# Composite convolution as three half-length products by column parity, with the differences and filter sums on VectorE

## The chip, the cores and the metric

One core of one Trainium2 chip. The metric is the device time in microseconds of one execution, launch to end; lower is better. The profile is of one execution of the same program.

## The reference, cut to what matters

`x` is (32 samples, 64 channels, 1024), `cond_512` a style vector of 128 per sample. Two levels follow each other, each a chain of four modulated convolutions over the columns, then a feed-forward part, with a residual:

```
for i, typ in enumerate(('same', 'upsample', 'same', 'downsample')):
    s = style @ mw[i].T + mb[i]                       # (B, 64) per layer
    weight = SCALE * w[i] * s[:, None, :, None]
    demod = rsqrt(sum(weight ** 2, axis=(2, 3)) + EPS)
    out = conv(out, weight * demod, typ) + b[i]       # 3 taps; blur by [1,3,3,1]/8 after up, before down
level 0: x1 = h + 2 * sum_k gate_k * B_k (A_k h)      # 64 adapters of rank 16, top 16 by a router, softmax gates
level 1: out = x1 + (h @ dequantised int4 weight) + bias
```

In both levels `h` stands for the conditioned tensor that enters the feed-forward part; the residual is taken from the level's input. All is float32 in the reference.

## The kernel before, in words

Columns are stored by parity: row p of a pair tile holds the 512 even and then the 512 odd columns. 32 samples make 16 pairs (`NPAIR`); a pair has samples a = 0 and 1. Channels are 64 (`C`), so 128 partitions are 64 channels x 2 column parities, and H = 512 is the length of a half row.

A product keeps float32 accuracy by splitting both operands in a high and a low part (`hi`, `lo`) and adding hi x hi, hi x lo and lo x hi: `products`, L168 to L175, three matmuls for each stationary tile. The high part is a ScalarE copy to fp32r, the low part a VectorE subtraction (`low`, L156 to L158).

The first convolution of a sample is `pe_layer1` (L620): 6 matmuls of 512 columns. ScalarE scales its result in PSUM and makes `h_hi` (`act_layer1`, L630), VectorE makes `h_lo` (`dve_layer1`, L639). The other three convolutions, with the two blurs, are folded per sample into one filter of 4 tiles: `pe_fold3` (L537) and `pe_fold2` (L571) compute the filters, `act_fold2` (L586) and `dve_fold2` (L598) make `e_hi` and `e_lo` and copy them to the other half of the partitions. `pe_cond` (L645) is the composite convolution: 4 tiles x 3 = 12 matmuls of 512 columns per sample, each tile against `h` shifted by one more column. `act_cond` (L654) scales it, adds the bias and writes the two edge columns, which come from a small side computation (`edge_tensor`, `edge_vector`) done once per level for all samples.

The work is ordered by hand, one program per engine, with semaphores between them. In the first level's step i (`first_step`, L1070, L1177, L1268) the convolutions of pair i + 1 are laced between the feed-forward matmuls of pair i: layer1, transposes (`pe_turn`), fold3, scores, 24 hidden matmuls, fold2, 24 hidden matmuls, convolution of sample 0, transposes of the gated tensor, convolution of sample 1, 48 adapter-output matmuls. In the second level's step (L1115 to L1127, L1220, L1330) there are 32 matmuls of `pe_quant` in place of them. VectorE's order in the second level is: fold-start lows, lows of the turned tensor, `h_lo` of sample 0, fold3 lows, `h_lo` of sample 1, reduction, `e_lo`, split of the next input (`dve_split`), row sum, residual. GpSimd adds the bias to the residual in the second level (L1040) and issues the stores of finished pairs and the loads of the residual's input. SyncE loads the input of a pair (`sp_load`, L931) as soon as the pair before has been split.

Each engine goes through its program strictly in order; a wait holds everything behind it on that engine. The start of each level (filters, tables, edges, and at level 0 the splitting of the adapter matrices) is straight code before the loops, in which pairs 0 and 16 are done, and pair 1 in an unrolled first step.

## Time and profile before

| | us |
|---|---|
| median of 3 runs | 992.88 |
| lowest and highest | 990.76, 996.49 |
| the profiled execution, its own time | 990.33 |
| its span, first to last instruction | 988.8 |
| mean granted TensorE clock in it | 0.978 |

Busy times are per engine; a matmul's duration includes its way through the array, so the spacing of starts, not the mean duration, is what one costs in a row of them. "Idle before" is the time in which the engine did nothing ahead of an instruction, and "<-" names what ended it. PEclk is the granted clock of TensorE: 1.00 is 2.4 GHz, 0.50 is 1.2 GHz. PE is TensorE, DVE VectorE, ACT ScalarE, POOL GpSimd, SP SyncE.

### The profile page before, as it was taken

The numbers are of one execution on the slowest core, as the hardware profiler recorded it, in microseconds if no ns is written. First come the engines' busy times: TensorE is split into PE (matmuls) and PEld (weight loads), VectorE is DVE, ScalarE is ACT, GpSimd is POOL, SyncE is SP. The second block draws the span as 40 slices with busy tenths as digits, with TensorE's granted clock in tenths as the row PEclk, the third lists the DMA queues.
The fourth block names the chain that finished last, engine by engine and source line by source line (L and its number), as shares of the span: only waits on it lengthen the run. The fifth ranks groups of instructions, "written<-read, shape, count | busy, mean of one in ns | idle before, by whom it ended". The sixth has DMA issues, their size and how long they took to land.

```text
span 988.8 us, 14065 instructions
## 1 busy us (share of the span) xinstructions
PE 940.2 (95%) x4636; PEld 792.4 (80%) x4636; DVE 558.3 (56%) x1133; ACT 376.2 (38%) x717; POOL 111.0 (11%) x141
## 2 busy tenths in 40 slices
PE   5899999999999999999999998839999999999997
PEld 4777888888888888888888887638888888888886
DVE  8894353353353354344344333966677767777774
ACT  2672243243243243233233221434554445444541
POOL 7100000000000000000000000710112111211121
PEclk8799999999999999999999999859999999999999
DMA  8701011011011011101101101331221222112211
GB/s 281 244 5 65 22 42 64 21 42 64 21 42 64 25 39 64 40 25 63 42 28 57 42 21 54 54 106 29 100 85 64 65 96 94 64 64 87 96 50 64
DMA packets 33567, 64.12 MB, mean 65 GB/s; under 512 B 12304, under 2 KB 13968, under 8 KB 33552
## 3 DMA queue, kind: packets, MB, share of 16 engines
q1 hardware_dynamic: 24480, 30.90, 10.6%
q0 software_dynamic: 9072, 33.03, 9.2%
q8 instruction: 7, 0.11, 0.0%
q14 instruction: 8, 0.07, 0.0%
HBM read 47.14 MB, written 16.78 MB: 65 GB/s over the span
## 4 chain that ended last, share of the span: by engine, by line
PE 88%; DVE 8%; issue 2%; ACT 1%; DMA 1%; POOL 0%; SPq 0%; POOLq 0%; DVEq 0%; ACTq 0%
PE conv_ps L172 9%; PE conv_ps L174 8%; PE conv_ps L173 8%; PE fold_ps L581 6%; PE prod_ps L743 6%; PE prod_ps L744 6%; PE prod_ps L745 6%; PE prod_ps L725 6%; PE prod_ps L726 6%; PE prod_ps L727 6%; PE prod_ps L824 6%; PE prod_ps L823 6%; PE fold_ps L548 3%; PE turn_ps L682 3%; PE turn_ps L704 1%
## 5 line engine op out<-in xcount | busy, mean ns | idle before, releaser
L158 DVE TENSOR_TENSOR h_lo<-conv_ps,h_hi 64x512 fp32r<-64x512 f32 x128 | 88.2, 689 | 47.3 <-ACT h_hi L637 46.4
L172 PE MATMUL conv_ps<-h_hi,e_hi 128*128 128x512 f32 x256 | 104.9, 410 | 2.4 <-issue 2.4
L657 ACT ACTIVATE cond<-conv_ps,bias,demod_tab 128x510 f32<-128x510 f32 x64 | 49.9, 779 | 144.7 <-PE conv_ps L174 132.7
L173 PE MATMUL conv_ps<-h_lo,e_hi 128*128 128x512 f32 x256 | 102.2, 399 | 0.0
L174 PE MATMUL conv_ps<-h_hi,e_lo 128*128 128x512 f32 x256 | 102.1, 399 | 0.0
L743 PE MATMUL prod_ps<-b_hi,xt 128*128 128x512 f32 x256 | 99.9, 390 | 2.3 <-DVE xt L158 2.3
L823 PE MATMUL prod_ps<-quant,xt_hi 128*128 128x512 f32 x256 | 100.3, 392 | 1.4 <-DVE xt_lo L158 1.4
L801 DVE SCALAR_TENSOR_TENSOR res<-prod_ps,norm,res 128x512 f32<-128x512 f32 x32 | 23.9, 750 | 137.3 <-PE prod_ps L745 137.3
L726 PE MATMUL prod_ps<-a_lo,xt 128*128 128x512 f32 x256 | 101.0, 395 | 0.0
L725 PE MATMUL prod_ps<-a_hi,xt 128*128 128x512 f32 x256 | 101.0, 394 | 0.0
L727 PE MATMUL prod_ps<-a_hi,xt 128*128 128x512 f32 x256 | 101.0, 394 | 0.0
L824 PE MATMUL prod_ps<-quant,xt_lo 128*128 128x512 f32 x256 | 100.2, 391 | 0.0
L744 PE MATMUL prod_ps<-b_lo,xt 128*128 128x512 f32 x256 | 99.6, 389 | 0.0
L745 PE MATMUL prod_ps<-b_hi,xt 128*128 128x512 f32 x256 | 99.6, 389 | 0.0
L688 ACT ACTIVATE xt<-turn_ps 128x512 fp32r<-128x512 f32 x32 | 17.4, 594 | 166.8 <-PE turn_ps L682 166.8
L158 DVE TENSOR_TENSOR xt<-turn_ps,xt 128x512 fp32r<-128x512 f32 x64 | 41.3, 686 | 60.5 <-ACT xt L755 45.1
L1020 POOL DMA_DIRECT2D x_after_first<-res x15 | 8.1, 537 | 512.8 <-DVE res L801 512.8
L172 PEld LDWEIGHTS conv_ps<-h_hi,e_hi 128*128 128x128 f32 x256 | 49.2, 192 | 12.9 <-issue 2.5
L743 PEld LDWEIGHTS prod_ps<-b_hi,xt 128*128 128x128 f32 x256 | 48.0, 188 | 12.7 <-DVE xt L158 2.7
L755 ACT ACTIVATE xt<-turn_ps 128x512 fp32r<-128x512 f32 x32 | 17.6, 596 | 106.4 <-PE turn_ps L734 106.4
L174 PEld LDWEIGHTS conv_ps<-h_hi,e_lo 128*128 128x128 f32 x256 | 48.9, 191 | 11.5
L173 PEld LDWEIGHTS conv_ps<-h_lo,e_hi 128*128 128x128 f32 x256 | 49.1, 192 | 10.2
(222 smaller groups left out, 1982.4 us busy)
## 6 DMA issues: line engine op xcount, KB each, us to landing
x_in<-in_x SPq DMA_DIRECT2D x64, 128.0 KB, 2.7
res<-in_x POOLq DMA_DIRECT2D x16, 512.0 KB, 3.6
x_after_first<-res POOLq DMA_DIRECT2D x16, 512.0 KB, 2.9
x_in<-x_after_first SPq DMA_DIRECT2D x64, 128.0 KB, 2.7
res<-x_after_first POOLq DMA_DIRECT2D x16, 512.0 KB, 3.5
out_x<-res POOLq DMA_DIRECT2D x15, 512.0 KB, 2.9
a_raw<-in_adapter_in SPq DMA_DIRECT2D x8, 512.0 KB, 8.1
b_raw<-in_adapter_out SPq DMA_DIRECT2D x8, 512.0 KB, 8.0
```

Of the source, the lines that this page charges most:

```text
L158: return nc.vector.tensor_tensor(out, whole, hi.bitcast(F32), ALU.subtract)
L172: nc.tensor.matmul(out, hi(w), moving_hi(i), start=(i == 0), stop=False)
L173: nc.tensor.matmul(out, hi(w), moving_lo(i), start=False, stop=False)
L174: last = nc.tensor.matmul(out, lo(w), moving_hi(i), start=False, stop=(i == n - 1))
L725: nc.tensor.matmul(prod_ps[n][:, :], bufs.xt_hi[:, k, :], bufs.a_hi[:, k, cols], start=(k == 0), stop=False)
L726: nc.tensor.matmul(prod_ps[n][:, :], bufs.xt_hi[:, k, :], bufs.a_lo[:, k, cols], start=False, stop=False)
L727: last = nc.tensor.matmul(prod_ps[n][:, :], bufs.xt_lo[:, k, :], bufs.a_hi[:, k, cols], start=False, stop=(k == KT - 1))
L743: nc.tensor.matmul(prod_ps[n][:, :], bufs.xt_hi[:, k, :], bufs.b_hi[:, k, cols], start=(k == 0), stop=False)
L744: nc.tensor.matmul(prod_ps[n][:, :], bufs.xt_hi[:, k, :], bufs.b_lo[:, k, cols], start=False, stop=False)
L745: last = nc.tensor.matmul(prod_ps[n][:, :], bufs.xt_lo[:, k, :], bufs.b_hi[:, k, cols], start=False, stop=(k == KT - 1))
L823: nc.tensor.matmul(prod_ps[n][:, :], bufs.xt_hi[:, k, :], bufs.quant[:, k, cols], start=(k == 0), stop=False)
L824: last = nc.tensor.matmul(prod_ps[n][:, :], bufs.xt_lo[:, k, :], bufs.quant[:, k, cols], start=False, stop=(k == KT - 1))
```

## The change

The composite convolution of a sample, 4 filter tiles over 512 columns, becomes three products of 2 filter tiles over 256 columns each. The result of layer1 is scaled into one scratch buffer in SBUF by column parity: even columns as "centre", odd columns as "odd". VectorE forms two differences, odd - centre and (odd by one) - centre, of 257 columns each. ScalarE copies the 771 columns of differences and centre to `h_hi`, VectorE takes the low part. The filters are built whole (not split) in a scratch that overlaps that data buffer, VectorE adds neighbouring filters (two sums), ScalarE makes the high and VectorE the low part of six tiles. TensorE computes the middle product (filter sums against the centre) into `fold_ps[a]` and the two others (filters against the differences) into the halves of `conv_ps[a]`. ScalarE scales the middle product and adds the bias, and VectorE joins: the two halves times the scale, plus the middle, written interleaved. ScalarE then writes the edge columns. All columns move by one place for that; the weights of the feed-forward parts are rolled by one row to match, and a rolled copy of the packed int4 weights is loaded too.

The input buffers `x_in` are gone: a pair is loaded into `x_raw`, which shares its place with `x_lo`, and the load waits for layer1 of the pair before. The stored intermediate gets two pad words per half row. Level 1's first weight loads are issued only after the last hidden product of level 0. In the second level's loop TensorE does fold3 first and fold2 before both halves of `pe_quant`; ahead of that loop pair 16's convolution stands before the edge layers.

```diff
         def pe_fold3(pe, c, bufs, first=False):
...
+                pe.wait_ge(S.middle_scaled, 2 * c)
...
         def act_fold2(act, c, bufs, first=False):
             act.wait_ge(S.fold2_done, c + 1)
+            act.wait_ge(S.layer1_ready, 2 * c + 2)
...
+            nc.scalar.activation(flat(whole[:, 0:E_PAIRS, :, 0:C]), blocks, ACT.Identity)
+            nc.scalar.activation(flat(whole[C:P, 0:E_PAIRS, :, C:P]), blocks[0:C, :, :], ACT.Identity)
+            nc.scalar.activation(flat(whole[0:C, 0:E_PAIRS - 1, :, C:P]), blocks[C:P, 2:2 * E_PAIRS, :], ACT.Identity)
+            nc.scalar.activation(whole[0:C, E_PAIRS - 1, :, C:P], zero_block[0:C, :, :], ACT.Identity).then_inc(S.fold2_whole, 1)
+
+        def dve_sum_taps(v, c, bufs):
+            v.wait_ge(S.fold2_whole, c + 1)
+            flat = lambda ap: ap.rearrange("p q a m -> p q (a m)")
+            nc.vector.tensor_tensor(flat(bufs.whole[:, 4:6, :, :]), flat(bufs.whole[:, 0:4:2, :, :]), flat(bufs.whole[:, 1:4:2, :, :]),
+                                    ALU.add).then_inc(S.taps_summed, 1)
+
+        def act_taps(act, c, bufs, first=False):
+            act.wait_ge(S.taps_summed, c + 1)
...
+            nc.scalar.activation(flat(bufs.e_hi[:, :, :, :]), flat(bufs.whole), ACT.Identity).then_inc(S.fold2_hi, 1)
+
+        def dve_taps(v, c, bufs):
+            v.wait_ge(S.fold2_hi, c + 1)
...
+            low(flat(bufs.e_lo[:, :, :, :]), flat(bufs.whole), flat(bufs.e_hi[:, :, :, :])).then_inc(S.fold2_ready, 1)
...
+        def act_layer1(act, c, a, bufs, first=False):
             act.wait_ge(S.layer1_done, 2 * c + a + 1)
+            if a == 1 or not first or bufs.first_sample:
+                act.wait_ge(S.layer1_ready, 2 * c + a)
...
+            nc.scalar.activation(even, by_parity[:, 0, :], ACT.Identity, bias=at(bias1, c, a, bufs), scale=at(scale1, c, a, bufs))
+            nc.scalar.activation(odd, by_parity[:, 1, :], ACT.Identity, bias=at(bias1, c, a, bufs), scale=at(scale1, c, a, bufs)).then_inc(S.layer1_scaled, 1)
+
+        def dve_differences(v, c, a, bufs):
+            v.wait_ge(S.layer1_scaled, 2 * c + a + 1)
+            centre = bufs.data[:, CENTRE:CENTRE + SPAN]
+            nc.vector.tensor_tensor(bufs.data[:, BEFORE:BEFORE + SPAN], bufs.data[:, ODD:ODD + SPAN], centre, ALU.subtract)
+            nc.vector.tensor_tensor(bufs.data[:, AFTER:AFTER + SPAN], bufs.data[:, ODD + 1:ODD + 1 + SPAN], centre, ALU.subtract).then_inc(S.differences, 1)
+
+        def act_layer1_hi(act, c, a, bufs):
+            act.wait_ge(S.differences, 2 * c + a + 1)
+            nc.scalar.activation(bufs.h_hi[a][:, :], bufs.data[:, 0:3 * SPAN], ACT.Identity).then_inc(S.layer1_hi, 1)
+
         def dve_layer1(v, c, a, bufs):
             v.wait_ge(S.layer1_hi, 2 * c + a + 1)
+            low(bufs.h_lo[a][:, :], bufs.data[:, 0:3 * SPAN], bufs.h_hi[a][:, :]).then_inc(S.layer1_ready, 1)
...
+            part(fold_ps[a][:, 0:T2], (5, 4), CENTRE).then_inc(S.middle_done, 1)
+            part(conv_ps[a][:, 0:T2], (3, 1), BEFORE)
+            part(conv_ps[a][:, T2:H], (2, 0), AFTER).then_inc(S.cond_done, 1)
...
+        def dve_join(v, c, a, bufs):
+            v.wait_ge(S.cond_done, 2 * c + a + 1)
+            v.wait_ge(S.middle_scaled, 2 * c + a + 1)
...
+            nc.vector.scalar_tensor_tensor(out=out, in0=both, scalar=at(demod_tab[:, LAYERS - 1, :], c, a, bufs), in1=middle,
+                                           op0=ALU.mult, op1=ALU.add).then_inc(S.joined, 1)
+
+        def act_ends(act, c, a, bufs):
+            act.wait_ge(S.joined, 2 * c + a + 1)
...
             def second_step(i, last):
                 c = i + 1
+                act_fold3(act, c, buf1)
+                act_layer1(act, c, 0, buf1)
                 act_turn(act, i, buf1)
+                act_layer1_hi(act, c, 0, buf1)
                 act_layer1(act, c, 1, buf1)
+                act_layer1_hi(act, c, 1, buf1)
                 act_fold2(act, c, buf1)
+                act_taps(act, c, buf1)
+                if not last:
+                    act_fold_start(act, c + 1, buf1)
+                for a in range(2):
+                    act_middle(act, c, a, buf1)
+                for a in range(2):
+                    act_ends(act, c, a, buf1)
...
             def second_step(i, last):
                 c = i + 1
+                dve_fold3(v, c, buf1)
                 dve_turn(v, i, buf1)
+                dve_differences(v, c, 0, buf1)
                 dve_layer1(v, c, 0, buf1)
+                dve_reduce(v, i, buf1)
+                dve_differences(v, c, 1, buf1)
                 dve_layer1(v, c, 1, buf1)
+                dve_sum_taps(v, c, buf1)
+                dve_taps(v, c, buf1)
                 if not last:
+                    dve_fold_start(v, c + 1, buf1)
                     split(c + 1, buf1)
                 dve_rowsum(v, i, buf1)
                 dve_second_residual(v, i, buf1)
+                for a in range(2):
+                    dve_join(v, c, a, buf1)
```

In the first level's step VectorE's new order is: fold-start lows, turned lows, differences and low of sample 0, fold3 lows, differences and low of sample 1, route, gate 0, filter sum, filter low, gate 1, lows of the gated turn, both joins, split of the next pair, residual.

## Rows read from the trace of the kernel before

**Rows 1.** Busy time of each engine over the span (the page's first part)

```profile
PE 940.2 (95%) x4636; PEld 792.4 (80%) x4636; DVE 558.3 (56%) x1133; ACT 376.2 (38%) x717; POOL 111.0 (11%) x141
```

**Rows 2.** Four stages: us; busy PE, PEld, DVE, ACT, POOL; granted clock; DMA share; GB/s

```profile
0.00:75.60 75.60, 56.20 (x252) 47.02 (x252) 65.06 (x151) 42.90 (x69) 20.66 (x37) 0.89 0.53 173
75.60:599.50 523.90, 523.84 (x2582) 440.47 (x2583) 219.70 (x506) 160.09 (x320) 14.91 (x28) 1.00 0.13 42
599.50:674.50 75.00, 51.94 (x245) 43.30 (x244) 49.08 (x112) 23.28 (x38) 22.92 (x31) 0.82 0.28 71
674.50:971.90 297.40, 297.40 (x1510) 253.09 (x1510) 217.75 (x357) 147.94 (x286) 49.01 (x42) 1.00 0.22 74
```

**Rows 3.** Chain that ended last, two first-level steps: start, us, what

```profile
310.26 1.06 PE fold_ps L548 x6
346.95 1.05 PE fold_ps L548 x6
```

**Rows 4.** TensorE's instructions, a first-level step: start, us, what

```profile
318.54 0.28 PE L581 MATMUL fold_ps<-r_lo,fold_hi 128*128 128x256 f32 x1
320.07 0.28 PE L581 MATMUL fold_ps<-r_hi,fold_lo 128*128 128x256 f32 x1
325.78 0.39 PE L172 MATMUL conv_ps<-h_hi,e_hi 128*128 128x512 f32 x1
328.57 1.04 PE L734 MATMUL turn_ps<-ident,cond 128*128 128x128 f32 x8
```

**Rows 5.** VectorE's groups of instructions, shapes kept apart: xcount, busy us, mean ns

```profile
L158 DVE TENSOR_TENSOR h_lo<-conv_ps,h_hi 64x512 fp32r<-64x512 f32 x128 | 88.2, 689 | 47.3 <-ACT h_hi L637 46.4
L158 DVE TENSOR_TENSOR e_lo<-fold_ps,e_hi 128x512 fp32r<-128x512 f32 x32 | 22.0, 686 | 6.8 <-ACT e_hi L593 6.7
L158 DVE TENSOR_TENSOR a_lo<-a_raw,a_hi 128x1024 fp32r<-128x1024 f32 x8 | 9.2, 1217 | 0.0
L605 DVE CAST e_lo<-e_lo 64x512 fp32r<-64x512 f32 x32 | 13.5, 423 | 1.1
L606 DVE CAST e_lo<-e_lo 64x384 fp32r<-64x384 f32 x32 | 11.3, 354 | 0.4
L801 DVE SCALAR_TENSOR_TENSOR res<-prod_ps,norm,res 128x512 f32<-128x512 f32 x32 | 23.9, 750 | 137.3 <-PE prod_ps L745 137.3
L815 DVE TENSOR_REDUCE sums<-cond 128x2 f32<-128x1024 f32 x16 | 19.5, 1219 | 0.5
```

**Rows 6.** ScalarE's groups of instructions, shapes kept apart

```profile
L560 ACT ACTIVATE r_hi<-fold_ps,scale 128x256 fp32r<-128x256 f32 x64 | 26.9, 472 | 3.2
L1167 ACT ACTIVATE wr<-wr_raw 128x512 fp32r<-128x512 f32 x1 | 0.6, 631 | 0.0
L902 ACT ACTIVATE a_hi<-a_raw 128x1024 fp32r<-128x1024 f32 x8 | 8.0, 1046 | 0.0
L661 ACT ACTIVATE cond<-cond_edge 128x2 f32 x58 | 11.6, 199 | 0.0
```

**Rows 7.** Timeline of a second-level step: hand-overs between engines

```profile
791.33 0.39 PE L172 MATMUL conv_ps<-h_hi,e_hi 128*128 128x512 f32 x1
791.70 0.78 ACT L657 ACTIVATE cond<-conv_ps,bias,demod_tab 128x510 f32<-128x510 f32 x1 [5.26 <-PE conv_ps L174]
804.55 0.60 ACT L593 ACTIVATE e_hi<-fold_ps 128x512 fp32r<-128x512 f32 x1 [2.52 <-PE fold_ps L581]
805.18 0.69 DVE L158 TENSOR_TENSOR e_lo<-fold_ps,e_hi 128x512 fp32r<-128x512 f32 x1 [0.48 <-ACT e_hi L593]
```

**Rows 8.** Timeline: GpSimd beside VectorE at the start, and GpSimd's bias addition later

```profile
16.54 1.27 POOL L354 TENSOR_TENSOR L_turn_out<-L_turn_raw 128x512 f32<-128x512 f32 x1
16.57 1.38 DVE L391 TENSOR_TENSOR demod_tab<-demod_tab,L_newton 128x128 f32<-128x128 f32 x1
811.94 1.23 DVE L847 TENSOR_TENSOR res<-res,scaled 128x1024 f32<-128x1024 f32 x1
821.13 2.40 POOL L1040 TENSOR_TENSOR res<-res,bias 128x1024 f32<-128x1024 f32 x1 [3.16 <-DMA res<-x_after_first]
```

More of the change, by code:

```diff
@@ L500, in at @@
             return tab[:, n:n + 1] if isinstance(n, int) else tab[:, bass.ds(n, 1)]
+        T2 = H // 2
+        SPAN = T2 + 1
+        BEFORE, AFTER, CENTRE, ODD = 0, SPAN, 2 * SPAN, 3 * SPAN
+        STEP = 2 * P
+        PARTS = 6
+        SHARED = PARTS * STEP
+        DATA = SHARED - ODD + 1
         def conv_buffers(b):
             T = lambda n, s, d=F32R: tensor(outer, n, s, d)
[L505 to L506 removed]
+            b.x_hi = [T(f"x_hi{a}", [P, H + 1]) for a in range(2)]
+            with ExitStack() as stage:
+                b.x_raw = [tensor(stage, f"x_raw{a}", [P, H + 1], F32) for a in range(2)]
+            b.x_lo = [T(f"x_lo{a}", [P, H + 1]) for a in range(2)]
+            b.h_hi, b.h_lo = [T(f"h_hi{a}", [P, 3 * SPAN]) for a in range(2)], [T(f"h_lo{a}", [P, 3 * SPAN]) for a in range(2)]
             b.v_hi, b.v_lo = T("v_hi", [P, DOWN_PAIRS, 2, C]), T("v_lo", [P, DOWN_PAIRS, 2, C])
             b.r_hi, b.r_lo = T("r_hi", [P, R_PAIRS, 2, C]), T("r_lo", [P, R_PAIRS, 2, C])
[L510 removed]
+            b.e_hi, b.e_lo = T("e_hi", [P, PARTS, 2, P]), T("e_lo", [P, PARTS, 2, P])
+            scratch = T("scratch", [P, DATA + 4 * SPAN + 1], F32)
+            b.whole = scratch[:, 0:SHARED].rearrange("p (q a m) -> p q a m", q=PARTS, a=2)
+            b.middle = [scratch[:, a * T2:(a + 1) * T2] for a in range(2)]
+            b.data = scratch[:, DATA:]
         def level_buffers(conv, L):
@@ L648, in pe_cond @@
                 pe.wait_ge(S.fold2_ready, c + 1)
             pe.wait_ge(S.layer1_ready, 2 * c + a + 1)
-            cut = lambda w: (lambda q: w[a][:, q:q + H])
-            products(conv_ps[a][:, :], (3, 2, 1, 0), tiles(bufs.e_hi[:, :, a, :]), tiles(bufs.e_lo[:, :, a, :]), cut(bufs.h_hi), cut(bufs.h_lo)).then_inc(S.cond_done, 1)
-        def act_cond(act, c, a, bufs):
-            act.wait_ge(S.cond_done, 2 * c + a + 1)
-            act.nop(nofuse=True)
-            nc.scalar.activation(bufs.cond[:, a, 1:H - 1], conv_ps[a][:, 1:H - 1], ACT.Identity, bias=at(bias4, c, a, bufs),
-                                 scale=at(demod_tab[:, LAYERS - 1, :], c, a, bufs))
+            cut = lambda w, first: (lambda u: w[a][:, first + u:first + u + T2])
@@ new lines, in pe_cond, with act_middle @@
+            part = lambda out, filters, data: products(out, filters, tiles(bufs.e_hi[:, :, a, :]), tiles(bufs.e_lo[:, :, a, :]),
+                                                       cut(bufs.h_hi, data), cut(bufs.h_lo, data))
+            part(fold_ps[a][:, 0:T2], (5, 4), CENTRE).then_inc(S.middle_done, 1)
+            part(conv_ps[a][:, 0:T2], (3, 1), BEFORE)
+            part(conv_ps[a][:, T2:H], (2, 0), AFTER).then_inc(S.cond_done, 1)
+        def act_middle(act, c, a, bufs):
+            act.wait_ge(S.middle_done, 2 * c + a + 1)
+            act.nop(nofuse=True)
+            nc.scalar.activation(bufs.middle[a], fold_ps[a][:, 0:T2], ACT.Identity, bias=at(bias4, c, a, bufs),
+                                 scale=at(demod_tab[:, LAYERS - 1, :], c, a, bufs)).then_inc(S.middle_scaled, 1)
@@ L1236, in _ @@
             v.sem_inc(S.scored, 1)
-            for a in range(2):
-                nc.vector.memset(x_in[a][0:C, H:H + 1], 0.0)
-                nc.vector.memset(x_in[a][C:P, 0:1], 0.0)
             def split(c, bufs, first=False):
@@ L1286, in first_step @@
                 dve_gated_turn(v, i, buf0)
+                v.wait_ge(S.gated_turned, 2 * i + 2)
+                for a in range(2):
+                    dve_join(v, c, a, buf0)
                 if not last:
```

249 lines of the change are left out of this document (134 added, 115 removed).

## The prediction

> **What bounds the kernel now.** I read the busy table first, then the busy time by stage, then the chain of waits, and last the instructions of one step on each engine. TensorE is busy 95% of a span of 988.8 us, VectorE 56%, ScalarE 38% [rows 1]. The stages tell more. In the first level's loop (75.6 to 599.5 us) and the second's (674.5 to 971.9) TensorE has no gap at all; in the start and in the change of levels it has, and there VectorE is nearly full: 65 of 75.6 us, 49 of 75 [rows 2]. So removed TensorE work pays only in the loops, and only while VectorE and ScalarE deliver in time. A first-level step takes 36.7 us [rows 3]; a second-level step 297.4 / 15 = 19.8 us, of which VectorE works 217.75 / 15 = 14.5 us [rows 2]. That second loop has the least room, and the change puts most of its new work on VectorE.
>
> **What TensorE saves.** The composite convolution of a pair is now 24 matmuls of 512 columns: 12 of them start 325.78 to 328.57, 0.2325 us each [rows 4]. The change issues 2 samples x 3 products x 2 filters x 3 = 36 matmuls of 256 columns. Fold2 has this form (full weights, 256 columns): 13 intervals in 1.53 us, 0.118 each [rows 4]. So 5.6 us become 4.2, 1.4 us per pair less. Weight loads hide at this spacing already in fold2, so I add nothing for them.
>
> **What VectorE gets, per pair.** A two-input fp32 operation takes 0.686 us for 512 elements and 1.217 for 1024 [rows 5], so 1.037 ns per element on 0.155. Removed: four halves of h_lo at 0.689, and e_lo with its two copies, 0.686 + 0.423 + 0.354 [rows 5]: 4.2 us. Added: four differences of 257 elements (0.42 each, 1.7), two lows of 771 (0.95, 1.9), the filter sum (0.69), one filter low of 1536 (1.75), two joins. A join is a scalar_tensor_tensor of 512 from PSUM like L801, 0.75 [rows 5]; its stride-2 write has no row: its ends are 0.75 and twice that, and I take 0.75, the row with the same sources and size. Together 7.5 us, net +3.3. In the second level VectorE's own work becomes 14.5 - 4.2 + 7.5 = 17.8 us, against TensorE's new 18.4. Busy time alone would just fit.
>
> **What ScalarE gets, and the trips.** The three copies over a pair's h become, per sample, two scaled copies of 256 (0.47, [rows 6]) and, after the differences, one high copy of 771, between 0.631 for 512 and 1.046 for 1024 [rows 6]: 0.84. The filters need four copies (0.60 [rows 7], 0.60, 0.50, 0.33 by size, overlapping slightly: 1.85) and a high copy of 1536 (0.63 + 1024 x 0.81 ns = 1.46). The sum is not the point, ScalarE has room; the order is. There is one data buffer, shared with the filter scratch: sample 1's scaled copies wait for sample 0's low, and the filter copies for sample 1's low. So VectorE stands while ScalarE answers. ScalarE-to-VectorE hand-overs cost little: e_hi ends 805.15, e_lo starts 805.18 [rows 7]; I take 0.05 each way, and 0.3 from TensorE to ScalarE (791.33 to 791.70 at most, [rows 7]).
>
> **One second-level step, along VectorE's queue.** The joins are now last in the queue, behind both residual parts, and everything of the next step hangs on them. After the second join: ends (0.2, [rows 6]) and ScalarE's two fold3 copies, which stand behind them, let VectorE wait 1.2. TensorE's layer1 of sample 0 waits for the first join's ends; layer1 (1.4), the transposes (0.9) and ScalarE's copies leave a wait of 0.9 before the turned lows. Each high copy of h: 0.84 + 0.15 = 1.0, twice. Sample 1's scaled copies hide behind the reduction of 1.22 us [rows 5]. The filter copies: 1.95. The filters' high copy: 1.6. Sum of waits 7.6 us; with the 17.8 of work 25.4 us per step. TensorE meanwhile waits some 4 us for the filters' low before the convolution and 3 us for the join before layer1; the convolution itself (4.2 us) runs beside VectorE's split, rowsum and residual (about 8 us) and is not on this cycle.
>
> **GpSimd.** The old h_lo and e_lo read PSUM and SBUF; the new differences and lows read SBUF twice. VectorE's 128x128 product of two SBUF tensors took 1.38 us beside a GpSimd operation of 1.27 that began 0.03 earlier; they end within 0.14 of each other [rows 8]; by size it is 0.29. In the second loop GpSimd's bias addition (2.40 us) starts 8.0 us after the last residual sum [rows 8], so in the new order from 6.6 to 9.0 us after the second join's end (the joins follow that sum with 1.4 us). Counted from there, VectorE waits 1.2, does the fold3 lows (0.9), waits 0.9, does the turned lows (1.3) and differences (0.8), waits 1.0, does the low (0.9) and the reduction (1.2), 0.3 of it overlapped: sample 1's differences are due at 7.9 and are held until 9.0, +1.1 us. The ends are 0 (no overlap) and 2.4 (it catches a low as well). I take 1.1: 26.5 us per step. The Trainium skill (SBUF — State Buffer, on the shared port pair) says a VectorE operation with two SBUF inputs and a GpSimd operation that reads SBUF exclude each other for a whole instruction, which speaks against this change; the row agrees. Without it the sum would be 1089, with it 1105.
>
> **First-level step.** The same trips, but 36.7 us to hide them. Route starts only when TensorE has summed the scores, then gate 0, the filter sum, ScalarE's 1.46 and the low of 1.75: counted from layer1, TensorE's score sum ends at 11.9 (its own queue, all matmuls at the present spacing), route takes 3.4 and gate 0 0.6, so the filter sum runs 16.0 to 16.7, the high copy to 18.2 and the low to 20.0. TensorE, whose queue is at the convolution at 19.4, waits 0.7. Joins (1.5) and the delayed split are covered by 10.9 us of adapter output. So 1.4 - 0.7 = 0.7 us less per step, 14 steps: -9 us. Ends: -19 (no wait) and +5.
>
> **Start and change of levels.** Pairs 0, 1 and 16 go through where VectorE is full. From scaled copy to filters' low the serial chain is 2 x (0.84 + 0.84 + 0.95) + 0.9 + 1.85 + 0.69 + 1.46 + 1.75 + hand-overs = 12.8 us, against some 4.5 before; with joins +9.5 where nothing fills the trips, less where nibbles, chunks or edge steps do. In the change of levels the convolution now stands ahead of the edge layers and of the joins, with TensorE at half clock (mean 0.82 in this stage, [rows 2]): 36 x 0.21 = 7.7 us. Taken: +8, +6 and +11 (there also the level-1 loads, issued only once the last hidden product is done, and one more load), together +25; ends 12 and 35. The end, 971.9 to 988.8 us [rows 2], from the last looped sum through GpSimd's store, load and bias, is as before. The other DMA edits (loads that wait for layer1, padded rows of 2 KB pieces) have 10 us or more ahead of the split: nothing, at worst within the range.
>
> **Sum.** The second loop starts with its joins done, so I count 14.5 steps: 14.5 x (26.5 - 19.8) = +97. With +25 and -9: +113 on 990.33, the profiled execution: 1103. The median shown, 992.88, lies 2.5 higher, so I say 1105.
>
> **Rivals.** (a) TensorE stays the bound, because ScalarE's trips are hidden after all (say the queues overlap more than the waits in the code let me see): -1.4 x 29 steps = -40, start and change +15 to +25, so about 970. For it: VectorE's 17.8 is below TensorE's 18.4. Against it: each wait named above is a semaphore in program order on one buffer; it decides once the waits sum to under 0.9 us per step instead of 7.6 (16 us of start, change and first level to win back over 14.5 steps). 6%, and 2% for waits of just about 0.9, which end within 0.5%. (b) The chain as above but GpSimd misses: 1089, 25%. (c) The chain, and TensorE's clock falls in its waits of 4 to 5 us per step: in the change of levels, with long waits, it was granted 0.82 [rows 2]; layer1 and the transposes at half speed lie on the cycle, up to +2.3 us per step, 1138. 15%. (d) My forecast, 52%. That the change does less than it says I exclude: the diff issues 36 x 256 columns.
>
> **Numbers.** Lower end: no GpSimd meeting (1089), trips 0.7 us shorter (-10), start and change +15 (-10), no wait in the first level (-10): 1060. Upper end: (c), 1138. A measurement of this kernel tells about 0.5% (5 us) from no change. Faster 6%, same 2%, slower 92%.
>
> **What would show it.** In the new profile: second-level steps of 25 to 27.5 us; TensorE idle there, waiting for e_lo before the convolution and for the conditioned tile's ends before layer1; VectorE waiting for ScalarE's h_hi, whole and e_hi for 1 to 2 us each; differences of 0.42 us, some stretched beyond 1 us under the bias addition; first-level steps of 36.0; convolution matmuls 0.118 apart. It is wrong if TensorE is gapless in the second loop, or if that loop's step is under 20 us.

## The result: 13% slower, as the chain of waits had it

The changed kernel takes 1121.4 us, median of 4 runs (1120.8 to 1123.6), beside 992.8 for the kernel before: a ratio of 1.129, 95% interval 1.126 to 1.133. Predicted were 1105 us, 1060 to 1138. The profiled execution took 1123.6 us with a span of 1122.1.

The busy table of the changed kernel answers to [rows 1]:

```profile
PE 956.1 (85%) x5020; PEld 828.2 (74%) x5020; DVE 669.8 (60%) x1209; ACT 429.3 (38%) x845; POOL 120.1 (11%) x143
```

TensorE falls from 95% to 85% of a longer span, and VectorE and ScalarE stay at 60% and below: this is what a loop looks like that hangs on hand-overs. Where the time is, the windows tell (us; busy PE, PEld, DVE, ACT, POOL; granted clock; DMA share; GB/s). They are cut at the second residual product of the first pair, at the same of the last looped pair, and at the first and the last looped row-sum copy (neg_sum), so each loop window holds 14 steps (the last of the second loop is shorter, because no further pair is split in it). First the changed kernel:

```profile
0.00:104.11 104.11, 71.85 (x325) 62.62 (x326) 73.10 (x141) 45.81 (x77) 22.25 (x39) 0.80 0.37 118
104.11:612.62 508.51, 500.15 (x2704) 427.89 (x2703) 259.05 (x542) 181.98 (x376) 19.41 (x28) 1.00 0.15 43
612.62:723.44 110.82, 74.41 (x345) 63.63 (x344) 63.47 (x136) 37.96 (x65) 22.84 (x31) 0.76 0.24 66
723.44:1100.20 376.76, 294.23 (x1571) 260.74 (x1569) 261.98 (x374) 160.51 (x319) 51.94 (x42) 0.88 0.18 57
1100.20:1122.10 21.90, 15.48 (x80) 13.31 (x80) 12.22 (x19) 3.03 (x8) 3.67 (x3) 0.90 0.20 72
```

and the kernel before, cut at the same instructions:

```profile
0.00:86.88 86.88, 67.42 (x301) 56.33 (x302) 68.13 (x156) 42.90 (x69) 20.66 (x37) 0.90 0.48 157
86.88:599.74 512.86, 512.86 (x2536) 431.36 (x2535) 216.63 (x501) 160.09 (x320) 14.91 (x28) 1.00 0.12 42
599.74:689.78 90.04, 66.98 (x324) 55.87 (x323) 59.70 (x130) 33.46 (x56) 22.92 (x31) 0.85 0.25 65
689.78:967.79 278.01, 278.01 (x1413) 237.02 (x1412) 203.16 (x333) 136.89 (x266) 49.01 (x42) 1.00 0.23 77
967.79:988.80 21.01, 14.91 (x68) 11.82 (x67) 10.65 (x16) 2.83 (x6) 3.48 (x3) 1.00 0.21 76
```

Start +17.2, first level -4.4, change of levels +20.8, second level +98.8, end +0.9: together the 133.3 us. TensorE worked without a gap in the old second loop (278.01 of 278.01 us); now it stands 82.5 of 376.8 us. A step of that loop has grown from 19.86 to 26.91 us by these windows; counted from filter low to filter low, without the short last step, the changed kernel has 27.13. Every step length below is the mean by the windows, unless it says "from filter low to filter low".

Here is one step of that loop on VectorE, from one filter low to the next (start, us, what, and in brackets the idle time before it and its releaser):

```profile
909.73 1.76 DVE L165 TENSOR_TENSOR e_lo<-scratch,e_hi 128x1536 fp32r<-128x1536 f32 x1 [1.63 <-ACT e_hi L633]
...
917.28 1.23 DVE L899 TENSOR_TENSOR res<-res,scaled 128x1024 f32<-128x1024 f32 x1
918.42 1.41 DVE L713 SCALAR_TENSOR_TENSOR cond<-conv_ps,demod_tab,scratch 128x512 f32<-128x512 f32 x2
921.58 0.88 DVE L589 SCALAR_TENSOR_TENSOR r_lo<-fold_ps,scale,r_hi 128x256 fp32r<-128x256 f32 x2 [1.75 <-ACT r_hi L584]
923.20 1.29 DVE L165 TENSOR_TENSOR xt_lo<-turn_ps,xt_hi 128x512 fp32r<-128x512 f32 x2 [0.74 <-ACT xt_hi L740]
...
926.07 0.96 DVE L165 TENSOR_TENSOR h_lo<-scratch,h_hi 128x771 fp32r<-128x771 f32 x1 [0.92 <-ACT h_hi L681]
926.95 1.21 DVE L867 TENSOR_REDUCE sums<-cond 128x2 f32<-128x1024 f32 x1
928.26 1.47 DVE L676 TENSOR_TENSOR scratch<-scratch 128x257 f32<-128x257 f32 x1
929.65 0.41 DVE L677 TENSOR_TENSOR scratch<-scratch 128x257 f32<-128x257 f32 x1
930.98 0.96 DVE L165 TENSOR_TENSOR h_lo<-scratch,h_hi 128x771 fp32r<-128x771 f32 x1 [0.92 <-ACT h_hi L681]
933.97 0.69 DVE L624 TENSOR_TENSOR scratch<-scratch 128x512 f32<-128x512 f32 x1 [2.02 <-ACT scratch L619]
936.29 1.76 DVE L165 TENSOR_TENSOR e_lo<-scratch,e_hi 128x1536 fp32r<-128x1536 f32 x1 [1.63 <-ACT e_hi L633]
```

From the first filter low to the second there are six waits, every one for ScalarE, 8.0 us together. The one stretched row is L676: the first difference of sample 1 takes 1.47 us, beside GpSimd's bias addition of 927.05 to 929.45; the second difference, behind it on L677, takes 0.41. All 64 on L676, ns min/median/max:

```profile
L676 DVE TENSOR_TENSOR scratch<-scratch x64: 417/427/2651, 27.8 to 1090.6; 128x257 f32<-128x257 f32 x64
```

TensorE in the same step: after the row sums it stands 5.3 us, and the convolution then runs 0.21 us apart, nearly twice the 0.118 of [rows 4], until it is back at 0.12 before its end.

```profile
905.75 0.50 PE L862 MATMUL turn_ps<-sums,spread 128*128 128x1 f32 x4
911.54 0.58 PE L179 MATMUL fold_ps<-h_hi,e_hi 128*128 128x256 f32 x1 [5.29 <-DVE e_lo L165]
911.92 0.41 PE L180 MATMUL fold_ps<-h_lo,e_hi 128*128 128x256 f32 x1
912.14 0.41 PE L181 MATMUL fold_ps<-h_hi,e_lo 128*128 128x256 f32 x1
...
917.66 0.28 PE L181 MATMUL conv_ps<-h_hi,e_lo 128*128 128x256 f32 x1
917.78 0.28 PE L179 MATMUL conv_ps<-h_hi,e_hi 128*128 128x256 f32 x1
```

So rival (c) came true in its first half: the granted clock falls to its lower level (0.50 from 911.5 to 914 us), once per step. It does so under the convolution, which takes 5.7 to 7.1 us in the 14 steps, and not under layer1 and the transposes, where (c) had put it: from layer1's first matmul to fold3's they take 3.87 us in all of them, at full clock. Whether the fall costs anything is the second experiment.

### The profile page after: what moved, and what is told of

It is laid out like the page before. It is cut to its first block and busy times, and to the rows that moved or that the text cites. A ratio compares the mean times of both kernels' runs of the same rounds, so it can differ in the third digit from the quotient of the medians.

```text
span 1122.1 us, 15246 instructions
## 1 busy us (share of the span) xinstructions
PE 956.1 (85%) x5020; PEld 828.2 (74%) x5020; DVE 669.8 (60%) x1209; ACT 429.3 (38%) x845; POOL 120.1 (11%) x143
## 5 line engine op out<-in xcount | busy, mean ns | idle before, releaser
L179 PE MATMUL fold_ps<-h_hi,e_hi 128*128 128x256 f32 x128 | 49.3, 385 | 106.4 <-DVE e_lo L165 106.4
L179 PEld LDWEIGHTS fold_ps<-h_hi,e_hi 128*128 128x128 f32 x128 | 31.7, 248 | 114.5 <-DVE e_lo L165 114.5
L165 DVE TENSOR_TENSOR h_lo<-scratch,h_hi 128x771 fp32r<-128x771 f32 x64 | 61.6, 962 | 72.4 <-ACT h_hi L681 72.4
L165 DVE TENSOR_TENSOR e_lo<-scratch,e_hi 128x1536 fp32r<-128x1536 f32 x32 | 56.3, 1758 | 52.2 <-ACT e_hi L633 52.2
L681 ACT ACTIVATE h_hi<-scratch 128x771 fp32r<-128x771 f32 x64 | 54.3, 848 | 80.5 <-DVE scratch L677 80.5
L179 PE MATMUL conv_ps<-h_hi,e_hi 128*128 128x256 f32 x256 | 82.0, 320 | 0.0
L180 PE MATMUL conv_ps<-h_lo,e_hi 128*128 128x256 f32 x256 | 81.9, 320 | 0.0
L181 PE MATMUL conv_ps<-h_hi,e_lo 128*128 128x256 f32 x256 | 81.3, 317 | 0.0
L703 ACT ACTIVATE scratch<-fold_ps,bias,demod_tab 128x256 f32<-128x256 f32 x64 | 34.7, 568 | 99.4 <-PE fold_ps L181 97.7
L179 PE MATMUL conv_ps<-x_hi,w_hi 128*128 128x512 f32 x128 | 56.2, 439 | 8.4 <-ACT cond L722 8.3
```

Of the source, the lines that this page charges most:

```text
L165: return nc.vector.tensor_tensor(out, whole, hi.bitcast(F32), ALU.subtract)
L179: nc.tensor.matmul(out, hi(w), moving_hi(i), start=(i == 0), stop=False)
L180: nc.tensor.matmul(out, hi(w), moving_lo(i), start=False, stop=False)
L181: last = nc.tensor.matmul(out, lo(w), moving_hi(i), start=False, stop=(i == n - 1))
```

## The experiments

The theory to test: in the second loop the step is VectorE's work plus its waits for ScalarE, set by the order of two queues and one shared buffer. Rivals: GpSimd's hold, the clock, VectorE's added work by itself, and TensorE's term.

**1. GpSimd's hold** (small_bias):

```diff
-                nc.gpsimd.tensor_tensor(buf1.res[:, :], buf1.res[:, :], buf1.bias[:, :], ALU.add).then_inc(S.biased, 1)
+                nc.gpsimd.tensor_tensor(buf1.res[:, 0:8], buf1.res[:, 0:8], buf1.bias[:, 0:8], ALU.add).then_inc(S.biased, 1)
```

> The changed kernel with GpSimd's bias addition of the second level cut to 8 of its 1024 columns (the bias of the other columns is left out); order, waits and transfers stay. Chain with GpSimd (my forecast): the first difference of sample 1 is no longer held, 0.42 us each time instead of 1.5 to 2.6, so a second-level step falls from 27.1 to about 25.5 us, 15 steps: 1121 becomes about 1098. If GpSimd does not matter (the stretch is covered by another wait): 1121, steps of 27.1. If the stretch is a wait for memory or for ScalarE, the difference stays long in the new trace.

1098.7 us (ratio 1.109, 1.107 to 1.111), second-level steps of 25.49 us from filter low to filter low, where the changed kernel has 27.13. The differences are flat:

```profile
L676 DVE TENSOR_TENSOR scratch<-scratch x64: 414/426/429, 27.4 to 1063.6; 128x257 f32<-128x257 f32 x64
```

GpSimd's hold costs 1.64 us per step, 23 us in all. What is left, 25.49, is the chain of work and trips that the prediction put at 25.4.

**2. The clock** (filler):

```diff
                 pe_rowsum(pe, i, buf1)
+                pe.wait_ge(S.layer1_ready, 2 * c + 1)
+                for k in range(20):
+                    nc.tensor.matmul(conv_ps[0][:, :], w1_hi[:, k % 2, :], buf1.h_hi[0][:, 0:H], start=True, stop=True)
                 pe_cond(pe, c, 0, buf1)
```

> The changed kernel with 20 matmuls of 512 columns more per second-level step (4.7 us), issued in TensorE's wait for the filters' low; their result is overwritten and never read. They keep the granted clock up. If the clock matters (rival c): the convolution takes 4.3 us instead of 6.7 and the step falls by up to 2.4 us, total down to about 1090. My reading of the profile after: VectorE reaches the joins only after the residual sum, just when the half-speed convolution ends, so nothing waits for the convolution; the trace shows full clock in the second loop and the time stays within 5 us of 1121.

1126.5 us (1.135, 1.132 to 1.138), no faster and if anything 5 us slower. The second loop has 0.97 of full clock instead of 0.88, the convolution has 0.12 us spacing throughout (4.3 to 4.4 us in every step), and TensorE then waits for the joins:

```profile
915.67 0.39 PE L179 MATMUL fold_ps<-h_hi,e_hi 128*128 128x256 f32 x1 [0.64 <-DVE e_lo L165]
...
923.88 0.50 PE L179 MATMUL conv_ps<-x_hi,w_hi 128*128 128x512 f32 x1 [2.60 <-ACT cond L722]
```

In this step VectorE's waits are those of the changed kernel (1.75, 0.73, 0.91, 2.02, 1.64). So the low clock under the convolution is free in this order. The run of experiment 1 says the same: its convolutions take 5.7 to 7.1 us and its steps 25.49 to 25.51, whichever of these it is.

But the filler did not only remove the low clock, it also moved it. In 6 of its 14 steps the clock is at the lower level behind TensorE's wait for the joins, under layer1 and the first transposes, 5.1 to 5.4 us for this stretch instead of 3.87, and there VectorE waits longer for the turned copies, 1.0 to 2.2 us instead of 0.74:

```profile
843.07 0.63 PE L181 MATMUL conv_ps<-x_hi,w_lo 128*128 128x512 f32 x1
845.45 1.29 DVE L165 TENSOR_TENSOR xt_lo<-turn_ps,xt_hi 128x512 fp32r<-128x512 f32 x2 [1.86 <-ACT xt_hi L740]
```

That is the second half of rival (c), and some of the 5 us: where the clock falls decides whether it costs.

**3. The joins ahead of the residual** (joins_early):

```diff
                 dve_rowsum(v, i, buf1)
-                dve_second_residual(v, i, buf1)
                 for a in range(2):
                     dve_join(v, c, a, buf1)
+                dve_second_residual(v, i, buf1)
```

> The changed kernel with the two joins of the second level's step put before the residual instead of behind it; nothing else moves. Chain of trips: the 1.75 us wait for fold3 and most of the 0.74 us wait for the turned copies hide behind the residual's 3.9 us; but the joins now come when the convolution at half clock is still running (it ends 3.6 us after the split, a join of sample 0 could start 1.0 us after it), so some 2.8 us of new waiting for the convolution replaces them: step 27.1 to 27.5 and 1121 becomes 1115 to 1130. If the convolution were not on the way here, the step would fall by 2.3 us, total 1087. This run with the one before last tells whether the clock is free of charge only because of the order.

1122.1 us (1.134, 1.131 to 1.136): the time expected, but not by the way expected. The waits came out as the expectation has them: those for fold3 and the turned copies (2.5 us) vanished, and waits for the low-clock convolution came in their place, 3.1 us per step in the mean, 2.25 in the step shown. All waits of VectorE together grew from 8.2 to 8.8 us per step. Here the low clock does cost: the steps run from 25.7 to 27.1 us as the convolution takes 5.7 to 7.1. Yet the loop's mean step fell, from 26.91 us in the changed kernel to 26.24, and that is GpSimd's: its addition now falls on the filter sum and lengthens it by 0.4 to 0.7 us, where it had held a difference for 1.6, and all differences are flat (427 ns at most):

```profile
908.66 0.75 DVE L713 SCALAR_TENSOR_TENSOR cond<-conv_ps,demod_tab,scratch 128x512 f32<-128x512 f32 x1 [0.84 <-PE conv_ps L181]
910.82 0.75 DVE L713 SCALAR_TENSOR_TENSOR cond<-conv_ps,demod_tab,scratch 128x512 f32<-128x512 f32 x1 [1.41 <-PE conv_ps L181]
...
925.78 1.28 DVE L624 TENSOR_TENSOR scratch<-scratch 128x512 f32<-128x512 f32 x1 [2.03 <-ACT scratch L619]
```

Of the 9 us won there 7 went back at the end: the last looped residual sum now stands behind the joins, and behind it GpSimd's store, load and bias, so the window after the last looped neg_sum has 29.1 us instead of 21.9. The rest is within the scatter of the start, which differs by up to 4 us between these versions though its code is the same (first residual product 101.5 to 105.7 us). The total alone would have told nothing.

**4. A data buffer for each sample** (two_buffers). Besides the second buffer, its waits and ScalarE's queue in the matching order:

```diff
                 dve_differences(v, c, 0, buf1)
-                dve_layer1(v, c, 0, buf1)
-                dve_reduce(v, i, buf1)
                 dve_differences(v, c, 1, buf1)
+                dve_layer1(v, c, 0, buf1)
                 dve_layer1(v, c, 1, buf1)
+                dve_reduce(v, i, buf1)
```

> The changed kernel with a data buffer for each sample in the second level, apart from the filter scratch: both samples' scaled copies and differences come first, then both high copies and lows, then the row sums; the filter copies no longer wait for sample 1's low. No VectorE work is removed. Chain of trips (my forecast): ScalarE's high copy of sample 1 and most of the filter copies (2.0 us) run beside VectorE's lows and row sums, some 3.5 to 5 us less per step, so a step of 22 to 23.5 us and 1121 becomes 1045 to 1070. If VectorE's work is what bounds the step: no change (1115 or more). If GpSimd's bias addition now falls on a longer operation, some 1 us of it is given back per step.

1073.2 us (1.083, 1.081 to 1.085), steps of 23.70, both just above what I expected: 3.2 us less per step with not one operation of VectorE removed. VectorE's waits fell by 3.1 us per step and GpSimd's hold stayed what it was, 1.6 to 1.7 us in the mean. The steps alternate between 25.0 and 22.7 us, for two reasons of about a microsecond each. GpSimd's addition falls in the long ones on the two lows, which take 1.83 us together where undisturbed (+2.2), and in the short ones on the filter sum (+1.1). And in the long ones the clock is at its lower level under layer1 (0.43 us from matmul to matmul instead of 0.23), so that VectorE waits 1.4 to 1.9 us for the turned copies instead of 0.79. The first three lines are of a long step, the last of a short one:

```profile
867.30 0.63 PE L180 MATMUL conv_ps<-x_lo,w_hi 128*128 128x512 f32 x1
870.15 1.29 DVE L165 TENSOR_TENSOR xt_lo<-turn_ps,xt_hi 128x512 fp32r<-128x512 f32 x2 [1.47 <-ACT xt_hi L743]
873.55 4.05 DVE L165 TENSOR_TENSOR h_lo<-data,h_hi 128x771 fp32r<-128x771 f32 x2
...
894.47 1.29 DVE L165 TENSOR_TENSOR xt_lo<-turn_ps,xt_hi 128x512 fp32r<-128x512 f32 x2 [0.79 <-ACT xt_hi L743]
```

**5 and 6. TensorE's part alone, and VectorE's work without the trips**, both made from the kernel before (short_matmuls, work_alone; both leave out the fourth tap). The edit to TensorE, which both have:

```diff
-            cut = lambda w: (lambda q: w[a][:, q:q + H])
-            products(conv_ps[a][:, :], (3, 2, 1, 0), ...)
+            for n in range(2):
+                cut = lambda w: (lambda q: w[a][:, q + n * 256:q + (n + 1) * 256])
+                last = products(conv_ps[a][:, n * 256:(n + 1) * 256], (3, 2, 1), ...)
```

> The kernel before with only TensorE's part of the change: the composite convolution of a sample as 18 matmuls of 256 columns instead of 12 of 512 (three of its four taps, in two halves; the fourth tap is left out), nothing else changed. The term of my sum: 1.4 us less per pair, 29 loop steps where TensorE is the bound: 992 becomes about 951. If the weight loads of the shorter matmuls don't hide, or another engine is close behind TensorE, the gain is under half of that (over 970).

> As the last one, and VectorE gets, in the second level's step, the work that the change adds net but none of its hand-overs: three additions of two SBUF tensors, 768, 1024 and 1024 columns, into an unused tile (0.95 + 1.22 + 1.22 = 3.4 us by the trace), which nobody waits for. If VectorE's added work itself bounds the changed kernel's step, this step goes to 24 us or more and the time to over 1020. If it is the trips (my forecast), VectorE's 17.9 us stay below TensorE's 18.4: the time is about 951, at most 970 with GpSimd's bias addition holding VectorE.

957.9 us (0.965, 0.962 to 0.967) and 963.9 (0.970, 0.967 to 0.973). TensorE's part does pay: 1.17 us per first-level step (35.46), 1.28 per second-level step (18.58). It is less than the 1.4 of the sum. In the second level the 36 matmuls take 4.41 us from their first start to the start of what follows, 0.1225 each where the sum had 0.118, and the 24 before took 5.69; in the first level another tenth is lost elsewhere in the step. In a row the intervals are 0.120:

```profile
320.78 0.28 PE L172 MATMUL conv_ps<-h_hi,e_hi 128*128 128x256 f32 x1
320.90 0.28 PE L173 MATMUL conv_ps<-h_lo,e_hi 128*128 128x256 f32 x1
...
322.82 0.28 PE L174 MATMUL conv_ps<-h_hi,e_lo 128*128 128x256 f32 x1
```

And 3.4 us more work for VectorE per second-level step (3.2 by its busy time), with nobody waiting for it, cost 0.3 us per step (18.86). The changed kernel adds 2.6 us by busy time, once GpSimd's hold is out of it (experiment 1). So VectorE's added work, as such, is not what made the changed kernel slow: its trips are, and GpSimd's hold for the 1.64 us of experiment 1.

**7 and 8. The same work, in an order that hides the trips** (trips_hidden, trips_hidden_vector_bias). On top of experiment 4:

```diff
-                dve_taps(v, c, buf1)
                 if not last:
-                    dve_fold_start(v, c + 1, buf1)
-                    split(c + 1, buf1)
+                    dve_split(v, c + 1, 0, buf1)
+                dve_taps(v, c, buf1)
+                if not last:
+                    dve_fold_start(v, c + 1, buf1)
+                    dve_split(v, c + 1, 1, buf1)
                 dve_rowsum(v, i, buf1)
                 dve_second_residual(v, i, buf1)
-                for a in range(2):
-                    dve_join(v, c, a, buf1)
```

with the joins inside the residual, between its zero-point part and its scaled part; in the second version the bias addition stands there too, on VectorE.

> The changed kernel with all of its work, two data buffers in the second level, and VectorE's queue there set in another order: split of sample 0 in the trip of the filters' high copy, joins before the residual's scaled part, which covers fold3's and the turned copies' trips. By the durations of the trace VectorE then waits under 1 us per step; with 17.8 us of work and GpSimd's hold of 1 to 2.4 us a step takes 19 to 20.5 us instead of 27.1 (23.9 with two buffers alone): 15 steps, 1121 becomes 1000 to 1025. If a wait that I don't see (the convolution at half clock ahead of the joins) takes its place, the step stays over 22 us and the time over 1045.

> As the last one, but the bias is added on VectorE (1.22 us more work per step) and GpSimd adds nothing in the second loop. If GpSimd's 2.4 us hold VectorE for longer than 1.2 us per step in the last run, this one is faster by the difference, up to 1.2 us x 15 = 18 us; if it holds less, slower by up to 18 us. Every operation of VectorE then shows its unstretched duration: differences 0.42, filter sum 0.69, lows 0.96.

1032.5 us (1.039, 1.036 to 1.042), steps of 20.98: a miss, above both the 19 to 20.5 and the 1025. The trips are hidden, but GpSimd's addition (it starts at 854.98) now falls on the filter low, alone 1.76 us, and the convolution that waits for this low makes the second join wait as well, 0.8 to 1.0 us in ten steps. In the other four, of which this is one, TensorE's clock falls under that convolution too (5.9 us instead of 4.4); the joins wait 2.2 to 2.3 together, and the step takes 22.1 us instead of some 20.8:

```profile
855.28 3.71 DVE L165 TENSOR_TENSOR e_lo<-scratch,e_hi 128x1536 fp32r<-128x1536 f32 x1 [0.45 <-ACT e_hi L633]
...
865.35 0.75 DVE L716 SCALAR_TENSOR_TENSOR cond<-conv_ps,demod_tab,scratch 128x512 f32<-128x512 f32 x1 [2.33 <-PE conv_ps L181]
```

With the bias on VectorE, 1.22 us more work, 1006.7 us (1.014, 1.010 to 1.017) and steps of 19.07: 26 us faster, more than the 18 I had allowed, because the hold had cost twice, in the low (2.0 us per step) and in the join behind the delayed convolution (1.25 us, now gone; the clock is full in all 14 convolutions). I had priced only the first.

**9. Filters in parts, x_hi on ScalarE** (filters_in_parts). The first edit is for both levels, with VectorE's low in the same two parts; the second (x_hi as a scaled copy of ScalarE in the second loop) is not shown:

```diff
-            nc.scalar.activation(flat(bufs.e_hi[:, :, :, :]), flat(bufs.whole), ACT.Identity).then_inc(S.fold2_hi, 1)
+            nc.scalar.activation(flat(bufs.e_hi[:, 0:4, :, :]), flat(bufs.whole[:, 0:4, :, :]), ACT.Identity).then_inc(S.fold2_hi, 1)
+            act.wait_ge(S.taps_summed, c + 1)
+            nc.scalar.activation(flat(bufs.e_hi[:, 4:6, :, :]), flat(bufs.whole[:, 4:6, :, :]), ACT.Identity).then_inc(S.fold2_hi, 1)
```

> The version with trips hidden and the bias on VectorE, and two more moves off VectorE's way: in both levels ScalarE copies the filters' first four parts before VectorE's sum is done and VectorE takes the low in two parts (ends 1.1 us sooner by the trace's durations), and in the second level's loop ScalarE makes x_hi (2 x 0.49 us off VectorE). Second level: VectorE's 19.0 us of work become 18.2, below TensorE's 18.4, so a step of 18.4 to 18.7 instead of 19.16: -7 to -11 us. First level: TensorE's wait of 0.60 for the filters' low is covered, 14 x 0.6 = -8: steps of 35.7. Total 1007 becomes 985 to 993. If the first level's step stays at 36.3, its wait was not for the low but for something behind it.

988.7 us (0.996, 0.994 to 0.998). First-level steps are 35.45 us, exactly those of the short matmuls alone (35.46): TensorE's wait for the filters' low was all that the first level had lost. The second level has 18.84, just above the 18.4 to 18.7 expected; TensorE is gapless there, but its step is 0.26 us longer than with the short matmuls alone, and where that lies stays open.

**10. The edges ahead** (edges_ahead), outside the loops; TensorE's queue there in the matching order, and the start's edits as the expectation lists them:

```diff
             dve_sum_taps(v, NPAIR, buf1)
+            edge_vector(v, 1, set1, 0)
             dve_taps(v, NPAIR, buf1)
-            for a in range(2):
-                dve_join(v, NPAIR, a, buf1)
+            edge_vector(v, 1, set1, 1)
             dve_nibbles(v, 4, 6)
-            edge_vector(v, 1, set1, 0)
-            edge_vector(v, 1, set1, 1)
-            dve_nibbles(v, 6, 7)
+            dve_join(v, NPAIR, 0, buf1)
             edge_vector(v, 1, set1, 2)
+            dve_join(v, NPAIR, 1, buf1)
+            dve_nibbles(v, 6, 7)
```

> As the last one, and outside the loops: in the change of levels the four edge layers are laced between filter sum, filter low, joins and convolution on both engines, instead of standing behind the joins (there VectorE waits 4.4 and 2.2 us for the half-speed convolution, and the edge chain of 20 us starts only then); in the start the edge step goes ahead of the filter sum, two adapter chunks between the joins, and ScalarE's fold-start copies ahead of two chunks and the table load. If the +11 and +14 of my sum are queue order, about 9 us come back in the change of levels and 3 to 5 in the start: 12 us less than the last run, 972 to 982, below the kernel before (992). If they are work and half clock, at most 3 us come back.

973.7 us, ratio 0.981 (0.979 to 0.983), with the whole computation: this version beats both kernels, the one before by 1.9%, clear of noise but small. Its windows:

```profile
0.00:99.09 99.09, 68.39 (x325) 58.39 (x326) 73.14 (x143) 46.08 (x79) 22.28 (x39) 0.84 0.39 124
99.09:595.44 496.35, 496.35 (x2704) 429.02 (x2703) 261.22 (x556) 183.26 (x390) 19.41 (x28) 1.00 0.15 44
595.44:683.19 87.75, 65.98 (x333) 56.18 (x332) 59.31 (x141) 38.54 (x68) 20.64 (x30) 0.84 0.31 83
683.19:947.09 263.90, 263.90 (x1583) 235.93 (x1583) 239.44 (x376) 175.94 (x360) 17.97 (x28) 1.00 0.25 82
```

TensorE is gapless again in both loops. The change of levels lost 13.4 us (101.1 to 87.8), more than the 9 expected; of the start only 0.8 came back of 3 to 5, and that is within its scatter of 4 us. So the loss in the change of levels was queue order. Most of the start's is not, or not the part that I moved; what else it is stays open.

**11. The transfers alone** (transfers_alone): the kernel before with padded rows, transfers in two pieces and the loads' new wait.

> The kernel before with only the transfers of the change: rows of the intermediate array padded to 2 x 514 words, so that residual store and load go as pieces of 2 KB, and the loads of the next pair wait for layer1 instead of the split. My sum puts nothing on it: 987 to 997, and the second level's residual load lands in 4.7 us instead of 3.5 as in the changed kernel if the padded pieces cause that; if that figure stays at 3.5, the longer landing comes from what runs beside it.

993.3 us, 1.0006 (0.999 to 1.002): nothing, as the sum had it. The residual load lands in 4.0 us there (3.5 before, 4.7 in the changed kernel), so pieces explain less than half of the longer landing.

**12. The bias back on GpSimd** in the fastest version (edges_ahead_gpsimd_bias):

> The version with the edges ahead, but with the bias addition of the second level back on GpSimd (as in both given kernels), so 1.22 us less work for VectorE per step. If GpSimd's 2.4 us addition holds VectorE's SBUF-only operations for its whole length, as the 3.7 us filter lows in the trips-hidden run suggest (1.76 alone), a step is 1 to 2 us longer than 18.85 and the time 15 to 30 us above 974; by work alone VectorE would have 17.0 us, TensorE would bound the step with 18.4 to 18.6, and the time would be 968 to 971.

980.3 us (0.987, 0.985 to 0.989), 6.7 above, steps of 19.05: between my two cases. The hold is there in full, 2.1 to 2.2 us in every step: in nine of 14 on the split's lows, which take 1.41 us alone, in five on a part of the filter low:

```profile
818.18 2.79 POOL L1118 TENSOR_TENSOR res<-res,bias 128x1024 f32<-128x1024 f32 x1 [3.14 <-DMA res<-x_after_first]
```

```profile
818.65 3.54 DVE L664 SCALAR_TENSOR_TENSOR x_lo<-x_raw,style_tab,x_hi 128x513 fp32r<-128x513 f32 x2
822.11 0.74 DVE L557 SCALAR_TENSOR_TENSOR v_lo<-down_T,scale,v_hi 128x192 fp32r<-128x192 f32 x2
```

but VectorE is busy 18.1 us of the 19.05, hold included, so 16.0 without it: it has some 3 us to spare (the 17.0 of my expectation was too much), and the hold eats most of that. Only 0.2 us per step comes through. The other 4 us of the total lie outside the loop; in the two profiles the change of levels differs most, 92.6 us against 87.8, and I didn't follow why.

## Why the prediction was right, point by point

**The bound.** Right: what TensorE saves in the second loop is lost as soon as the trips leave it idle, and they did. Experiments 5 and 6 separate the two.

**TensorE's term.** Mis-sized: 1.4 us per pair, measured 1.17 and 1.28. The numbers in the sum give only 1.33 (24 x 0.2325 less 36 x 0.118), and 0.118 was the spacing of one short burst. The sign "0.118 apart" did not come out either: 0.120 in the first level, 0.213 in most of the second level's convolution.

**One second-level step.** The order of the waits is as predicted. The step without GpSimd was put at 25.4 us and measured 25.49, but so close by luck: the waits are 8.2 us in place of 7.6 (the six long ones 8.0), and VectorE's busy time is 17.3 in place of 17.8. Two single terms were off: the wait for fold3's copies is 1.75 us, not 1.2 (each sample's ends are two instructions of 0.20, and the copies stand behind four of them), and the scaled copies take 0.56, not 0.47. The contiguous middle copy of the same size takes as long (L703, 568 ns), so it is what these copies share against the row of 0.47, a bias operand and a float32 output instead of fp32r, and not the stride of two. The join's stride of two cost nothing, as taken; its group on VectorE (count, busy us, mean ns, idle before):

```profile
L713 DVE SCALAR_TENSOR_TENSOR cond<-conv_ps,demod_tab,scratch 128x512 f32<-128x512 f32 x64 | 46.6, 749 | 14.6 <-PE conv_ps L181 14.5
```

TensorE's waits were put at 4 us before the convolution and 3 before layer1. They are 3.7 to 5.9 (mostly above 5) and 0 to 1.3 us: the convolution at the lower clock takes some 2 us longer than the 4.2 of the sum and uses up most of the second wait. In the step shown it issues its last matmul at 918.02 and VectorE begins the joins at 918.42, so it is off the cycle by little.

**GpSimd.** The mechanism was right, its size not: 1.64 us per step instead of 1.1, with holds of 1.0 to 2.2 us in single steps. The residual load lands in 4.7 us (median) instead of 3.5, and the addition starts 9.1 us after the last residual sum (mean of 14 steps) instead of 7.9. So it runs from 7.8 to 10.2 us behind the second join and not from 6.6 to 9.0, and the difference, due at 8.4 and not 7.9, stands in it for longer. Of the later landing the padded pieces explain less than half (experiment 11); the rest stays open. The Trainium skill (SBUF — State Buffer, section "SBUF: two separate sides") says that of a VectorE operation with two SBUF inputs and a GpSimd operation that reads SBUF, the one that starts first keeps the other out for its whole instruction. The traces agree where GpSimd starts first, on a difference (up to 2.65 us instead of 0.42), on lows (4.05 instead of 1.83) and on a filter low (3.71 instead of 1.76).

**The first level.** Term -9, measured -4.4; steps of 36.32 us, not 36.0. TensorE's saving is 1.17, and the wait for the filters' low costs more than it shows. It stands as 0.59 us, but in a row this matmul would have started 0.23 us after the one before and its successor 0.12 later; here they are 1.00 and 0.22. Together that is 0.87 us, just what experiment 9 won back (36.32 to 35.45):

```profile
304.68 0.40 PE L779 MATMUL prod_ps<-a_hi,xt 128*128 128x512 f32 x1
305.68 0.39 PE L179 MATMUL fold_ps<-h_hi,e_hi 128*128 128x256 f32 x1 [0.59 <-DVE e_lo L165]
305.90 0.28 PE L180 MATMUL fold_ps<-h_lo,e_hi 128*128 128x256 f32 x1
```

So 1.17 - 0.87 = 0.3 us per step, 14 steps. The sum had 1.4 - 0.7: the forecast of the wait was right, its price and the saving were not.

**Start and change of levels.** Term +25. Measured +17.2 for the start against +14, a difference within the start's scatter of 4 us. The +20.8 of the change of levels holds half a second-level step (3.6), so +17 against +11. I had seen that the edge layers now stand behind the convolution, but priced the convolution and not the chain of 20 us that begins only after it.

**The sum.** 1103 against 1123.6 for the profiled run: second loop 5, change of levels 6, first level 5, start 3, end 1 short. All errors have one sign, so none cancels another between the stages; within the second-level step, as said, two do. The centre was 16 us low on a loss of 129, and the time lies inside the range because the chain of waits makes up most of that loss.

**The rivals.** (a), 970, needed the trips hidden; once they are, and the bias addition is off GpSimd (experiments 7 to 10), the same products give 974. (b) is experiment 1: 1098.7, predicted 1089. (c): the clock falls each step, but under the convolution, where it costs nothing in this order. Its price is real where it lands on layer1, up to 1.3 us more waiting per step in experiments 2 and 4; the 2.3 us that the prediction had for it were seen nowhere. That it missed layer1 in the changed kernel I had no ground to know.

## What to carry to other kernels

When a change trades a bound engine's work for work on another, price the hand-overs before the work: here 3.4 us of work without hand-overs cost 0.3 us per step, while the changed kernel, with less net work but six waits for ScalarE and a hold by GpSimd, has steps 7 us longer. Ask of each wait what else the waiting engine could do in it; two buffers, a new order of the queues and two operations moved to other engines turned a loss of 13% into a gain of 1.9% with the same arithmetic. Look where the third engine's SBUF operations fall, since they move with every reordering.

## What the runs showed of the hardware beyond what I expected

GpSimd's addition of 2.4 us holds VectorE's operations with two SBUF inputs for up to 2.2 us, and what waits behind VectorE pays again: moving 1.22 us of work onto VectorE won 26 us in one order and 7 in another. Behind idle spells of about 5 us per step TensorE ran at the lower of its two levels (matmuls of 256 columns 0.213 us apart, 0.12 otherwise) in the convolution that follows, and filler in the spell kept the level up there. What this costs depends on where it lands: nothing under a convolution that nobody waits for, about 1 us per step where it fell on layer1 and the transposes (5.4 us instead of 3.9), 1.3 on a convolution ahead of the joins (steps of 22.1 us instead of 20.8). And a wait costs TensorE more than its idle time: 0.87 us for a gap of 0.6.
